# Local transformers of an eight-sublayer network: 32-query blocks, values stationary in 64x64 tiles, mask added by VectorE, values moved tile by tile

## What is computed

```python
DEPTH, HEADS, DIM_HEAD, WINDOW = 6, 16, 64, 32
def shift_tokens(t):                       # the upper half of the channels comes from the token before
    a, s = jnp.split(t, 2, -1)
    return jnp.concatenate([a, jnp.pad(s, ((0, 0), (1, 0), (0, 0)))[:, :-1]], -1)
def local_attention(q, k, v):              # blocks of 32 queries see their own block of keys and the one before
    ...
    bk2, bv2 = (look(bk), look(bv))
    mask = (it < jb) | (it > jb + w) | (jb == -1)
    sim = jnp.where(mask, -big, jnp.einsum('bhwie,bhwje->bhwij', bq, bk2) * QK_SCALE)
    return jnp.einsum('bhwij,bhwje->bhwie', jax.nn.softmax(sim, -1), bv2)
def attn_layer(x, Wqkv, qs, ksc, Wo):
    q, k, v = jnp.split(x @ Wqkv, 3, -1)   # 3 x 1024 columns
    q, k = l2norm(q) * qs, l2norm(k) * ksc # by head, then rotary embedding with a scale
    return local_attention(q, k, v).reshape(b, n, 1024) @ Wo
def ffn_layer(x, g, bln, W1, b1, W2, b2):  # layer norm, 341 gated channels, exact GELU
    a, gate = jnp.split(xn @ W1 + b1, 2, -1)
    return a * gelu(gate) @ W2 + b2
```

## Time and profile before

| | |
|---|---|
| three runs | 4340.34 us median, 4339.49 to 4340.35 |
| the profiled execution | span 4339.8 us from the first to the last instruction |
| PE busy, share of the span | 3995.2 us, 92% |
| DVE, ACT, POOL busy | 3715.0, 3380.3, 3380.2 us: 86, 78, 78% |
| TensorE clock granted | 0.957 of 2.4 GHz as a mean over the span |
| the two local transformers | slices 5 to 19 and 22 to 36 of the page's 40 |

### The profile page before, as it was taken

The page is one execution under the profiler, slowest core; times in us unless marked ns, Lnnn a source line. Parts: engine busy times, 40 slices in busy tenths (PEclk is TensorE's granted clock), DMA queues, the critical chain, the costliest instruction groups (busy, mean ns, idle before and its releaser), DMA issues. The chain is left out here.

```text
span 4339.8 us, 130231 instructions
## 1 busy us (share of the span) xinstructions
PE 3995.2 (92%) x46283; PEld 2655.5 (61%) x46283; DVE 3715.0 (86%) x12505; ACT 3380.3 (78%) x10657; POOL 3380.2 (78%) x4196
## 2 busy tenths in 40 slices
PE   6888799999999999999767999999999999996686
PEld 2333357767767767766553677767776776763464
DVE  6999789999999999999476999999999999974646
ACT  5888489999999999999414999999999999983122
POOL 3999698888888888888296888888888888861313
PEclk7999899999999999999897999999999999997887
DMA  1000101111111111111002111111111111100000
GB/s 28 1 1 1 46 24 31 41 31 36 41 27 49 31 34 44 26 34 27 15 1 53 31 27 41 36 41 31 36 41 27 51 29 29 37 24 3 6 3 10
DMA packets 78571, 122.04 MB, mean 28 GB/s; under 512 B 26024, under 2 KB 47204, under 8 KB 77924
## 3 DMA queue, kind: packets, MB, share of 16 engines
q1 hardware_dynamic: 77924, 113.71, 10.3%
HBM read 35.56 MB, written 1.05 MB: 8 GB/s over the span
## 5 line engine op out<-in xcount | busy, mean ns | idle before, releaser
L1095 POOL TENSOR_TENSOR local_qk<-local_qk,local_rb 128x512 f32<-128x512 f32 x768 | 975.7, 1271 | 224.2 <-DVE local_rb L1485 210.1
L1365 ACT ACTIVATE local_pr<-local_tb,local_nmax 128x96 f32<-128x96 f32 x3072 | 995.0, 362 | 68.7 <-DVE local_nmax L1501 67.1
L1191 PE MATMUL local_pj<-local_wqkv,local_xs 128*128 128x512 f32 x1536 | 808.4, 619 | 31.8 <-DVE local_rb L1485 17.8
L1101 POOL TENSOR_TENSOR local_qk<-local_qk,local_rinv 128x512 f32<-128x512 f32 x768 | 786.6, 1045 | 7.5
L1501 DVE CUSTOM_DVE_ANT_0 local_tb<-local_tb,local_mask 128x96 f32<-128x96 f32 x3072 | 689.2, 290 | 46.5 <-PE local_tb L1213 43.7
L1365 ACT ACTIVATION_READ_ACCUMULATOR local_pr<-local_tb,local_nmax 128x1 f32 x3072 | 703.3, 229 | 0.0
L1117 POOL TENSOR_TENSOR local_pr<-local_pr,local_rsum 128x384 f32<-128x384 f32 x768 | 622.4, 826 | 36.5 <-DVE local_rsum L1507 36.5
L1482 DVE TENSOR_TENSOR local_qk<-local_pj,local_rope 128x512 f32<-128x512 f32 x768 | 523.6, 682 | 62.8 <-ACT local_sq L1348 44.1
L1348 ACT ACTIVATE local_sq<-local_pj 128x512 f32<-128x512 f32 x768 | 462.2, 627 | 123.3 <-PE local_pj L1191 119.0
L1485 DVE TENSOR_TENSOR local_rb<-local_pj,local_rope 128x512 f32<-128x512 f32 x768 | 523.2, 681 | 2.8 <-POOL local_qk L1095 2.8
L1492 DVE TENSOR_REDUCE local_ss<-local_sq 128x8 f32<-128x512 f32 x768 | 512.0, 678 | 2.6 <-ACT local_sq L1348 0.8
(11 more groups left out here) (425 smaller groups left out, 7954.8 us busy)
## 6 DMA issues: line engine op xcount, KB each, us to landing
local_v<-local_v SPq DMA_DIRECT2D x288, 256.0 KB, 3.9
local_wqkv<-L_ffn_Wqkv_dram SPq DMA_DIRECT2D x72, 256.0 KB, 4.7
local_wo<-L_ffn_Wo_dram SPq DMA_DIRECT2D x12, 512.0 KB, 4.0
local_w<-L_ffn_W_dram SPq DMA_DIRECT2D x12, 341.0 KB, 4.8
mamba_parts<-mamba_in_low SPq DMA_DIRECT2D x24, 64.0 KB, 2.0
local_w<-L_ffn_W_dram SPq DMA_DIRECT2D x12, 128.0 KB
y_dram<-store_xtok SPq DMA_DIRECT2D x4, 256.0 KB, 2.9
local_oT<-rope_dram SPq DMA_DIRECT2D x2, 256.0 KB, 2.7
```

Source lines behind the costliest of these rows:

```text
L1095: nc.gpsimd.tensor_tensor(qk[:, u, :], qk[:, u, :], rb[:, u % 2, :], ALU.add).then_inc(s["summed"], 1)
L1101: nc.gpsimd.tensor_tensor(heads8(qk[:, u, :]), heads8(qk[:, u, :]), r, ALU.mult).then_inc(s["scaled"], 1)
L1191: nc.tensor.matmul(bank[:, :], xs[:, par, u // 4 * P:(u // 4 + 1) * P], wqkv[:, dep % 2, u % 4 * BANK:(u % 4 + 1) * BANK], start=True, sto ...
L1365: ins = nc.scalar.activation(pr[:, (NU * c + k) % PR_RING, i, WIN:WIN + KW], scores[:, i * KW:(i + 1) * KW], ACT.Exp, scale=-1.0, bias=nma ...
```

## The change

- The attention works on blocks of 32 queries against 64 keys (QB = 32, KW = 64). `score` has 2 steps of 64 matmuls in tiles of 64 rows by 32 columns, `turn_probs` 2 steps of 16 transposes, `weigh` 2 steps of 64 matmuls with a stationary tile of 64 keys by 64 value channels and 32 query columns moving. `weigh` writes a pair of the `tb` banks instead of a bank of its own; the bank that this frees is `fa`, a second one for the projections of the FFN and the output.
- The values of a window lie in `v` or in `vw`, which SyncE fills tile by tile: 6 transfers for the first tile of 128 tokens and 8 for the second.
- `maxima` is an addition of the mask over 512 columns within the scores' bank, and a reduction, four times a sequence. The multiplication with the inverse sum (`scale_p`) goes from POOL to DVE, the copy of the values from ACT to DVE, the copy of the outputs from DVE to ACT.
- The stream is kept skewed, 257 columns a sequence with the lower channel half one column later, so that `shift_in` and the shifted residual fall away. `out_project` and `down` are made in two halves of 64 output channels over 257 columns, 32 and 12 passes in all; the bias b2 is a row of `w2`.
- The layer norm's inverse root is taken by POOL in the same 14 steps as that of the queries and keys (two columns more), and `spread_root` (POOL) stands where `spread_std` was.
- The lags are shorter (4 iterations beyond the last sequence instead of 6), and every engine's list is new.
- The normalisation ahead of each local transformer writes the skewed stream in pieces of half the partitions.

```diff
 
 POOL_STEPS = 1 + 3 * 4
-STD_STEPS = 1 + 3 * 3
-
-V_BLOCK = (3, 0, 2, 1)
+ROOT_LEAD = 3
+
 SEQS = DEPTH * B
...
-
-
-PAIRS_OF_BANKS = [("qk", 2, 2), ("probs", 3, 2), ("qk", 2, 3), ("probs", 3, 3), ("probs", 2, 0), ("score", 2, 1),
-         ("score", 2, 2), ("score", 2, 3), ("qk", 1, 0), ("qk", 1, 1), ("probs", 2, 1), ("score", 1, 0)]
...
-        def couple(kk):
-
-            return kk // 2, kk % 2
+        def window(par, block, h):
+
+            t, at = divmod(block, BLOCKS)
+            own = slice(h * HALF, (h + 1) * HALF)
+            if at == 1 + 2 * h:
+                return v[own, par, t, h, :, :]
+            if at % 2:
+                return vw[own, par, t, :, :]
+            return vw[own, par, (4 if at == 0 else 2) + t, :, :]
...
-            def move_v(b, par, _):
-
-                sp.wait_ge(s["v_ready"], V_UNITS * b + V_UNITS)
-                need(sp, s["pv_ready"], COUPLES * (b - 1))
-                for place, row, source, source_row in ((3, QB, 0, 0), (2, 0, 0, QB), (2, QB, 1, 0)):
-                    sp.dma_start(v[row:row + QB, par, place, :, :], v[source_row:source_row + QB, par, source, :, :]).then_inc(s[f"v_moved{b % 2}"], 16)
+            def move_v(b, par, t):
+
+                sp.wait_ge(s["v_ready"], V_UNITS * b + 2 * t + 2)
+                need(sp, s["pv_ready"], TILES * (b - 2) + t + 1)
+                moved = s[f"v_moved{par}{t}"]
+                for h in range(2):
+                    row, other = h * HALF, (1 - h) * HALF
+                    sp.dma_start(vw[row + QB:row + 2 * QB, par, 4 + t, :, :], v[0:QB, par, t, h, :, :]).then_inc(moved, 16)
+                    if t:
+                        sp.dma_start(vw[row:row + QB, par, 5, :, :], v[3 * QB:P, par, 0, h, :, :]).then_inc(moved, 16)
+                    sp.dma_start(vw[row:row + HALF, par, t, :, :], v[other:other + HALF, par, t, h, :, :]).then_inc(moved, 16)
+                    sp.dma_start(vw[row:row + HALF, par, 2 + t, :, :], v[QB:3 * QB, par, t, h, :, :]).then_inc(moved, 16)
...
             def iteration(run):
-                run(move_v, 3, 0)
-                run(next_wqkv, 3, 0)
-                run(next_w1, 5, 0)
-                run(next_w2, 5, 0)
-                run(next_wo, 4, 0)
+                run(move_v, 0, 0)
+                run(next_wqkv, 0, 0)
+                run(move_v, 0, 1)
+                run(next_w1, 3, 0)
+                run(next_w2, 3, 0)
+                run(next_wo, 2, 0)
...
-            def norm_p(c, par, k):
-                pool.wait_ge(s["sum_inv"], COUPLES * c + k // 2 + 1)
-                at = pr[:, (NU * c + k) % PR_RING, :, WIN:WIN + KW]
-                nc.gpsimd.tensor_tensor(at, at, view(rsum[:, k // 2, k % 2, 0:1], [[1, 4], [0, KW]]), ALU.mult).then_inc(s["weighted"], 1)
+            def spread_root(e, par, _):
+                pool.wait_ge(s["root_steps"], ROOT_ALL * (e + ROOT_LEAD + 1))
+                pool.wait_ge(s["var_ready"], e + 1)
+                nc.gpsimd.tensor_tensor(work[:, :].rearrange("p (t c) -> p t c", t=TILES), view(net.ident[:, :], [[0, TILES], [1, P]]),
+                                        view(rinv[:, 2 * 2 * HEADS:NR], [[1, TILES], [0, P]]), ALU.mult).then_inc(s["diag_ready"], 1)
...
-                col = 2 * INNER + j % 2 * BANK
-                nc.tensor.matmul(bank[:, :], xs[:, par, j // 2 * P:(j // 2 + 1) * P], wqkv[:, dep % 2, col:col + BANK],
+                heads = view(wqkv[:, dep % 2, 2 * INNER:2 * INNER + 1], [[2 * DH, PAIRS], [1, DH]], j % 2 * DH)
+                nc.tensor.matmul(bank[:, :], stream[:, b % B, j // 2 * P:(j // 2 + 1) * P], heads,
...
-            def score(c, par, kk):
-                t, half = couple(kk)
-                sc = free_pair("score", c, kk)
-                if kk == 0 and c == 0:
+            def score(c, par, t):
+                sc = free_pair("score", c, t)
+                if t == 0 and c == 0:
                     pe.wait_ge(s["pad_ok"], 1)
-                if kk % 2 == 0:
-                    pe.wait_ge(s["qk_copied"], QK_UNITS * c + 4 * t + 4)
-                for i in range(4):
-                    for h, low in ((0, 0), (1, 1), (0, 1), (1, 0)):
-                        own, p, q = slice(h * DH, (h + 1) * DH), 4 * half + i, QB * (2 * t + low)
-                        ins = nc.tensor.matmul(sc[h][low * QB:(low + 1) * QB, i * KW:(i + 1) * KW], qT[own, par, p, q:q + QB],
-                                               kT[own, par, p, q:q + KW], start=True, stop=True)
+                pe.wait_ge(s["qk_copied"], QK_UNITS * c + 4 * t + 4)
+                for p in range(PAIRS):
+                    for i in range(BLOCKS):
+                        for h in range(2):
+                            own, q = slice(h * DH, (h + 1) * DH), t * P + i * QB
+                            ins = nc.tensor.matmul(sc[h][i * QB:(i + 1) * QB, p * KW:(p + 1) * KW], qT[own, par, p, q:q + QB],
+                                                   kT[own, par, p, q:q + KW], start=True, stop=True)
                 ins.then_inc(s["scored"], 1)
 
-            def turn_probs(c, par, kk):
-                banks = free_pair("probs", c, kk)
-                pe.wait_ge(s["weighted"], NU * c + 2 * kk + 2)
-                for h in range(2):
-                    for i in range(4):
-                        for low in range(2):
-                            rows, at = slice(low * QB, (low + 1) * QB), (4 * h + i) * QB
-                            ins = nc.tensor.transpose(banks[low][:, at:at + QB], pr[rows, (NU * c + 2 * kk + h) % PR_RING, i, :], net.ident[rows, rows])
+            def turn_probs(c, par, t):
+                banks = free_pair("probs", c, t)
+                pe.wait_ge(s["p_scaled"], 4 * c + 2 * t + 2)
+                for p in range(PAIRS):
+                    for low in range(2):
+                        rows = slice(low * HALF, (low + 1) * HALF)
+                        ins = nc.tensor.transpose(banks[low][:, p * HALF:(p + 1) * HALF],
+                                                  pr[rows, (TILES * c + t) % PR_RING, p, :, :].rearrange("q h k -> q (h k)"), net.ident[rows, rows])
                 ins.then_inc(s["probs_turned"], 1)
 
-            def weigh(c, par, kk):
-
-                t, half = couple(kk)
-                pe.wait_ge(s["probs_copied"], NU * c + 2 * kk + 2)
-                if kk == 0:
-                    pe.wait_ge(s[f"v_moved{c % 2}"], 48 * (c // 2) + 48)
-                need(pe, s["o_copied"], COUPLES * c + kk)
-                for i in range(4):
-                    for low in range(2):
+            def weigh(c, par, t):
+
+
+                ob = free_pair("weigh", c, t)
+                pe.wait_ge(s["probs_copied"], 4 * c + 2 * t + 2)
+                pe.wait_ge(s[f"v_moved{par}{t}"], MOVES[t] * (c // 2 + 1))
+                for i in range(BLOCKS):
+                    for p in range(PAIRS):
                         for h in range(2):
-                            ins = nc.tensor.matmul(ob[h * DH:(h + 1) * DH, i * P + low * QB:i * P + (low + 1) * QB],
-                                                   v[:, par, V_BLOCK[2 * t + low], 2 * (4 * half + i) + h, :],
-                                                   prT[:, kk % PT_RING, low, (4 * h + i) * QB:(4 * h + i + 1) * QB], start=True, stop=True)
+                            col, at = (h + p) % 2 * DH, p * HALF + i % 2 * QB
+                            ins = nc.tensor.matmul(ob[h][col:col + DH, p // 2 * P + i * QB:p // 2 * P + (i + 1) * QB],
+                                                   window(par, BLOCKS * t + i, h)[:, p, :], prT[h * KW:(h + 1) * KW, t, i // 2, at:at + QB],
+                                                   start=True, stop=True)
                 ins.then_inc(s["pv_ready"], 1)
...
                 for j in range(4 * part, 4 * part + 4):
-                    ins = nc.tensor.matmul(fb[:, 0:L], wo[:, j, :], oT[:, j, :], start=(j == 0), stop=(j == INNER // P - 1))
+                    for h in range(2):
+                        own = slice(h * HALF, (h + 1) * HALF)
+                        ins = nc.tensor.matmul(fa[own, 0:L + 1], wo[:, j, own], oT[:, j, 1 - h:L + 2 - h], start=(j == 0), stop=(j == INNER // P - 1),
+                                               skip_group_check=True)
...
                 pe.wait_ge(s["squared2"], e + 1)
                 for t in range(2):
-                    ins = nc.tensor.matmul(fb[:, L + t:L + t + 1], sq2[:, t * P:(t + 1) * P], net.mean[:, :], start=True, stop=True)
+                    ins = nc.tensor.matmul(fb[:, L + t:L + t + 1], work[:, t * P:(t + 1) * P], net.mean[:, :], start=True, stop=True)
-                for t in range(2):
-                    ins = nc.tensor.matmul(fb[:, t * P:(t + 1) * P], net.ones[:, :], diag[:, t, :], start=True, stop=True)
-                ins.then_inc(s["spread"], 1)
+                nc.tensor.matmul(fb[:, L:2 * L], net.ones[:, :], work[:, :], start=True, stop=True).then_inc(s["spread"], 1)
...
                 for j in range(3):
```

(5 more changed lines are left out.)

632 lines of the change are left out of this document (286 added, 346 removed).

## The result

The changed kernel takes 4692.9 us (median of four runs, 4676.1 to 4705.0) against 4340.4: 1.081 times as long, 95% interval 1.078 to 1.083. The forecast was 4132 with a range of 4050 to 4300. It has the wrong sign, and by much: the loss is 353 us. All times here are medians of executions in the faster of the chip's two states; one execution of run 7, with 11208.6 us, was in the slower state and is left out.

The account below looks back on a forecast made before the run. TensorE, never idle, was taken as the bound: 32.65 - 1.2 - 0.9 - 0.3 = 30.25 us a sequence, 30.65 with 0.4 for handovers; 4339.8 - 212.6 for two local transformers + 5 for normalisation = 4132 us, range 4050 to 4300.

Parts of the forecast that it names:

- TensorE's own steps: PE's steps a sequence: 32.65 less 1.2 for transposes, 0.9 for scores, 0.3 for weighing, giving 30.25 us.
- the upper end that I had written down: Score step on PE: 1.47 us if each burst kept the 0.082 of four; 1.2 was taken.
- the 0.4 of waits: Allowance on PE for late handovers from other engines: 0.4 us a sequence.
- From the period to the time: Each local transformer takes 50.07 periods less 6 us: 1528.6 us at 30.65, 106.3 less than before.
- Rivals C and D: D: column halves of out_project and down don't overlap, +4.9 us a sequence, 4623 us, chance 0.07. For C see rival C.
- rival C: Small matmuls on PE cost by their start: 39.1 us a sequence, 4979 us; chance 0.10 including the weighing's upper end.
- VectorE, ScalarE, GpSimd: Busy sums a sequence of 27.2, about 26.5 and about 22.5 us, all under PE's 30.25, so none becomes the bound.
- The transfers: SyncE's 14 transfers a sequence in place of 3 overlap and are read almost two iterations later: no cost.
- The handovers: PE waiting at spread, the last weighing or the third projection on shorter lags: 0.4 us a sequence.
- Rival B: Handovers bind, or eight tiles don't start in 0.054 us: periods of 31.2 to 32.3, 4190 to 4300 us, chance 0.21.
- the sum for PE: PE's own steps added up: 30.25 us a sequence, to which only 0.4 was added for the period of 30.65.

Follow-up runs that it names:

- run 7: Changed kernel with score and weigh steps cut in halves, other steps between, and probabilities and values in bf16 for the weighing: 4267.4 us, 0.983 of the kernel before.
- run 3: Changed kernel without the 14 value transfers a sequence, windows that need them reading zeros: 4678.9 us, 1.078 of the kernel before.
- run 4: Kernel before, with 20 more steps of 128 small score passes, back to back without waits, at the end of each local transformer: 4489.7 us.
- runs 6 and 7: The first: changed kernel with value projections between turn_probs, score and weigh, and bf16 probabilities and values, 4257.0 us, 0.981. The second: see run 7.
- run 8: Kernel before, with every score matmul of 96 columns written as two of 48: 4479.7 us, 1.032 of before.
- run 1: Changed kernel with the first two value projections moved between turn_probs, score and weigh on TensorE: 4514.2 us, 1.040 of the kernel before.
- runs 9 to 12: Changed kernel, second tile's steps rearranged, VectorE's first value copy earlier: score and weigh cut, weigh cut, uncut, uncut with ScalarE's bias_xn first: 4382.4, 4380.7, 4377.3, 4377.3 us.

## Why the prediction was wrong, step by step

*TensorE's own steps: right but for one.* The forecast had 30.25; the undisturbed steps sum to 31.0. `weigh` takes 2.00 (2.0 forecast), `out_project` 3.58 (3.5), `down` 1.36 (1.4), `turn_probs` 0.6 twice (the same). `score` was mis-sized: 1.41 in place of 1.2, at the upper end that I had written down, 0.42 a sequence. The rest, 0.3 in all, stands in the projections. With 31.0 and the 0.4 of waits the same working gives about 4210. *From the period to the time: right.* 50.07 x 36.44 - 6 is 1818.6, and local0 took 1819.2.

*Rivals C and D: decided against.* The column halves do overlap. A score pass costs 1.413 / 128, 11 ns on average, under the 25.6 of its step before; so rival C's mechanism was not at work. The Trainium skill's rule behind it (page "TensorE: Matmul & The Clock Gate", section "Wait — 56ns, not 53.3ns?": start to start never below about 25 ns) does not agree with this 11 ns, an average over passes in eight tiles. In the burst of run 4, though, 128 passes in 3.75 us are 29 ns a pass. Small passes were dear after all, for another reason: 2.0 of these us are passes at the low clock, and the rest is the stop.

*VectorE, ScalarE, GpSimd: near.* 704.9, 669.8 and 570.7 us in 24.7 sequences are 28.5, 27.1 and 23.1, against 27.2, 26.5 and 22.5. None of them is the bound.

*The transfers: right*, at next to no cost (run 3). *The handovers:* 0.4 was put down, 0.35 measured, at the first projection, ahead of which I expected none (I had named `spread`, `weigh` and the third projection); that the sizes agree is luck. Rival B's mechanism shows only with most of the stops out of the way: 1.3 to 1.4 in runs 6 and 7, periods of 31.7, inside its range of 31.2 to 32.3, but of kernels with a cheaper weighing.

*The step that failed* is the one from the sum for PE, 30.25, to the period, 30.65: it adds 0.4 for handovers and nothing else, and so takes for granted that TensorE can start its passes as fast as the array takes them. I multiplied passes (696 a sequence in place of 452) by nanoseconds and never counted the instructions, which come in packets over a DMA queue. The row was on the page: 370 packets in 4340 us, one in 11.7, harmless as a mean. What was not looked at is the densest stretch: 544 instructions in 4.1 us, where 256 in 3.5 to 4.0 is what the burst shows can be sustained. The stops cost 3.0 us a sequence. *The clock* was a second missing term: with a TensorE that never idles it stays at 1.00, and I kept it there for a kernel in which it idles 2 us at a time. It cost another 1.8. None of the rivals had either term.

The Trainium skill has the mechanism (page "Runtime: NRT & Kernel Launch", section "Instruction fetch mechanics"): instructions are refilled in blocks of 16 KiB, 256 instructions, by a queue of the sequencer's own. The packets here agree. It adds that crossing a block boundary is mostly hidden; the stops of 1.4 to 2.1 us, one in each portion of 256 of the burst, say otherwise for dense streams of small passes.

## What to carry to other kernels

Before splitting matmuls into smaller tiles, count the instructions of each stretch (here four for an fp32 matmul) and set them against the time of the stretch; the mean over the iteration says nothing. A stop in the middle of a step, with cause "issue", at the same place of a 256-instruction grid, is the supply; then the order is the first thing to change: long passes put between the dense steps, with one copy moved, gave back 316 of 353 us here, while TensorE's own steps went from 31.0 to 31.1. And price an idle TensorE twice: once for the stop, once for the slow clock behind it.

## What the runs showed of the hardware

- TensorE's instructions came in packets of 256, each 0.9 to 1.8 us on the queue. Under constant demand (run 4) one portion of 256 took 3.5 to 4.0 us, with the DMA engines otherwise idle. After quiet, 376 instructions went through in that burst before the first stop. In run 8, 320 in 3.4 us did not stop the engine.
- Every stop for instructions of over 0.25 us ended 1.2 to 1.7 us after the end of a packet, in the changed kernel and in all the runs.
- Without the 14 value transfers of a sequence the DMA share was 0.04 in place of 0.20, and the time 4679 in place of 4693 us: they slow neither the packets nor the engine by more than that.
- The granted clock fell to 1.2 GHz behind stops, and stayed there while TensorE was busy again (102 of 900 us in the changed kernel). No length of a stop separates the cases: it fell behind stops of at most 1.3 us in run 1 (24 of 900 us), not behind one of 2.04 in the changed kernel, nor behind those of up to 1.4 us in runs 9 to 12.
- 64x32 tiles over 64 columns ran at 11 ns a pass on average, 64x64 tiles over 32 columns at 15.6. Splitting 96 columns into two of 48 in the same tile made the step 0.36 us dearer.
